# Edge sums of a graph transformer: masked out of PSUM by ScalarE, added in one VectorE operation; sort steps two slots apart

## What is computed

```
q, k, v = xp @ Wq, xp @ Wk, xp @ Wv                      # xp: normed rows with position and degree terms
att  = clip(einsum('ehd,ehd->eh', q[dst], k[src]) / scale, -50, 50)
ex   = exp(att - m[dst])
s    = segment_sum(ex, dst)                              # and the 6250 self edges
aggr = segment_sum(v[src] * ex / s[dst], dst)
x    = x + aggr @ Wo;   x = x + gelu(layernorm(x) @ W1) @ W2
```

## Time and profile before

| | us |
|---|---|
| median of 3 runs (3809.33 to 3823.78) | 3817.89 |
| the profiled execution, whole | 3814.57 |
| its span, first to last instruction | 3812.6 |
| granted TensorE clock, mean | 0.888 |

### The profile page before, as it was taken

The page is one execution under the profiler, slowest core; times in us unless marked ns, Lnnn a source line. Parts: engine busy times, 40 slices in busy tenths (PEclk is TensorE's granted clock), DMA queues, the critical chain, the costliest instruction groups (busy, mean ns, idle before and its releaser), DMA issues.

```text
span 3812.6 us, 74017 instructions
## 1 busy us (share of the span) xinstructions
PE 3120.4 (82%) x25398; PEld 2506.9 (66%) x25705; DVE 2896.4 (76%) x6187; ACT 1821.4 (48%) x4404; POOL 2513.6 (66%) x2470
## 2 busy tenths in 40 slices
PE   4984688888898888888887688888888888888887
PEld 3753566667676666776776476666666676766665
DVE  8995678777777877878787387778777777777776
ACT  1331245445354544545555345554555555555555
POOL 1007777677676766767676477776677777777772
PEclk6785789899898989989999799889998989999997
DMA  3024455445454544545454355554555555555552
GB/s 85 23 74 141 117 153 167 138 147 169 127 171 132 171 144 140 165 137 165 143 174 139 103 163 171 169 168 145 159 176 159 164 168 165 176 169 170 165 169 77
DMA packets 427248, 558.53 MB, mean 146 GB/s; under 512 B 78472, under 2 KB 345440, under 8 KB 426676
## 3 DMA queue, kind: packets, MB, share of 16 engines
q0 software_dynamic: 117504, 321.02, 28.7%
q1 hardware_dynamic: 301862, 225.47, 19.6%
q10 hardware_dynamic: 7506, 7.20, 0.6%
HBM read 527.98 MB, written 25.44 MB: 145 GB/s over the span
## 4 chain that ended last, share of the span: by engine, by line
PE 44%; DVE 25%; issue 8%; ACT 7%; POOL 6%; DMA 5%; SPq 2%; DVEq 1%; another core or an unknown queue 0%; POOLq 0%; ACTq 0%
PE psum L952 12%; PE psum L1042 6%; POOL kv_ring L1965 5%; PE psum L993 4%; PE psum L1026 4%; DVE att L1683 4%; PE psum L1063 2%; DVE scratch L1674 2%; PE psum L1009 2%; DVE work L1378 2%; DVE kv_ring L1395 2%; DMA q_win<-q_table 2%; PE psum L1123 2%; PE psum L970 2%; DVE scratch L1698 2%
## 5 line engine op out<-in xcount | busy, mean ns | idle before, releaser
L1965 POOL DMA_INDIRECT kv_ring<-kv_table,src_idx x1840 | 1878.1, 1021 | 732.9 <-issue 543.8
L1228 ACT ACTIVATE scratch<-psum 128x512 f32<-128x512 f32 (+1 forms) x1228 | 679.5, 568 | 553.0 <-PE psum L970 201.0
L1965 POOL DMA_INDIRECT arena<-kv_table,src_idx x608 | 617.2, 1015 | 273.5 <-issue 179.8
L952 PE MATMUL psum<-arena 128*128 128x256 f32 x2156 | 673.1, 435 | 73.1 <-ACT scratch L1228 43.9
L1239 ACT COPY arena<-psum 128x512 f32<-128x512 f32 x616 | 327.3, 532 | 580.5 <-PE psum L952 577.9
L993 PE MATMUL psum<-q_win,scratch 64*128 64x128 f32 x4896 | 410.0, 314 | 169.1 <-DVE scratch L1674 80.4
L952 PEld LDWEIGHTS psum<-arena 128*128 128x128 f32 x2156 | 422.9, 216 | 177.1 <-ACT scratch L1228 58.3
L1683 DVE TENSOR_REDUCE att<-scratch 128x64 f32<-128x1024 f32 (+1 forms) x460 | 536.0, 1165 | 0.1
L993 PEld LDWEIGHTS psum<-q_win,scratch 64*128 64x128 f32 x4896 | 346.8, 214 | 263.7 <-issue 166.5
L1009 PE MATMUL psum<-scratch 128*64 128x136 f32 x4896 | 373.2, 297 | 17.4 <-ACT work L1322 6.3
L1674 DVE TENSOR_TENSOR scratch<-psum,kv_ring 128x1024 f32<-128x1024 f32 x230 | 280.3, 1219 | 139.6 <-DMA kv_ring<-kv_table,src_idx 92.4
(11 more groups left out here) (252 smaller groups left out, 4725.0 us busy)
## 6 DMA issues: line engine op xcount, KB each, us to landing
arena<-kv_table SPq DMA_DIRECT2D x154, 896.0 KB
kv_ring<-kv_table,src_idx POOLq DMA_INDIRECT x1840
q_win<-q_table SPq DMA_DIRECT2D x612, 32.0 KB
work<-kv_table SPq DMA_DIRECT2D x98, 128.0 KB
q_win<-q_table SPq DMA_DIRECT2D x154, 64.0 KB
arena<-kv_table,src_idx POOLq DMA_INDIRECT x608
work<-q_table SPq DMA_DIRECT2D x98, 64.0 KB
kv_table<-work SPq DMA_DIRECT2D x49, 128.0 KB, 2.1
```

The source lines that it names most:

```text
L952: mm = e.matmul(to[:, t % 2 * 2 * D:(t % 2 + 1) * 2 * D], hot_source[:, t * P:(t + 1) * P], source_rows[:, t, :], start=True, stop=True)
L1228: e.activation(to[:, at:at + width], apart[k % FILL_BANKS][:, 0:width], ACT.Relu, bias=1.0, scale=-1.0).then_inc(apart_read, 1)
L1965: e.indirect_dma_start(kv[m % RING_KV][:, t, :], None, kv_table[l], bass.IndirectOffsetOnAxis(ap=src_idx[:, c * T + t:c * T + t + 1], axis ...
```

## The change

1. ScalarE gets `mask_sums`: for a chunk it waits for the sums, and writes sums times mask for both rows to a new tile `masked` (two buffers of 2 x 136 columns in `arena`), with two ACTIVATE operations. This stands in slot 2u+4 for unit u, behind the exp of unit u+2.
2. `add_sums` of a chunk is one TENSOR_TENSOR over both rows, 272 columns, `acc` plus `masked`, and moves from slot 2u+3 to slot 2u+5. Block adds keep slot 2u+3. The order of the adds is written out (`add_order`), and each waits for the one before.
3. `bank_free` of a bank that held a chunk's sums waits for `sum_masked` in place of `acc_added`.
4. Node steps of tiles fed by chunks start two slots later; each layer's list is two slots longer.
5. From sort 1 on, steps 5 to 18 of a sort are two slots apart. Sort 5 then stands in slots 194 to 231.

```diff
-        ready = 2 * LAYERS[l].last_unit(j) + 4 - SUMS
+        ready = 2 * LAYERS[l].last_unit(j) + (4 if j >= LAYERS[l].jb else 6) - SUMS
...
+SORT_EVERY = 2
...
             slots.setdefault(u, []).append((s, k))
-            u += 1
             if k in SORT_BANKED:
-                slots.setdefault(u, []).append((s, -k))
+                slots.setdefault(u + 1, []).append((s, -k))
+            u += SORT_EVERY if s and 5 <= k < SORT_STEPS - 4 else 1
...
-    return max(2 * LAYERS[l].nu + 2, len(node_steps(l)))
+    return max(2 * LAYERS[l].nu + 4, len(node_steps(l)))
...
-                if name == "edges":
+                if name == "edges" and LAYERS[l].is_block(j):
                     e.wait_ge(acc_added, adds[unit(l, j)])
+                elif name == "edges":
+                    e.wait_ge(sum_masked, 2 * (chunk(l, LAYERS[l].units[j][1]) + 1))
...
+        def mask_sums(e, l, u):
+
+            n, i = unit(l, u), LAYERS[l].units[u][1]
+            m = chunk(l, i)
+            e.wait_ge(edge_summed, n + 1)
+            if m >= 2:
+                e.wait_ge(acc_added, adds[chunk_unit(m - 2)])
+            for k in range(2):
+                e.activation(masked[:, m % 2, k, :], edge_sum(l, u), ACT.Identity, scale=in_block[:, k, i:i + 1]
+                             ).then_inc(sum_masked, 1)
...
                         make_exp(e, l, u)
+                    if slot % 2 == 0 and 2 <= u < LAYERS[l].nu + 2 and not LAYERS[l].is_block(u - 2):
+                        mask_sums(e, l, u - 2)
                     for fill_of in fills[2:]:
...
             what, i = LAYERS[l].units[u]
+            if adds[n] > 1:
+                e.wait_ge(acc_added, adds[n] - 1)
             if what == "chunk":
+                m = chunk(l, i)
                 block = e.value_load(block_ring[0:1, i:i + 1], min_val=0, max_val=RING_W - 1)
-            e.wait_ge(edge_summed, n + 1)
-            if n >= 1:
-                e.wait_ge(acc_added, adds[n - 1])
...
-                for k in range(2):
-                    row = two[:, k, :]
-                    e.scalar_tensor_tensor(out=row, in0=of_edges, scalar=in_block[:, k, i:i + 1], in1=row, op0=ALU.mult,
-                                           op1=ALU.add).then_inc(acc_added, 1)
+                e.tensor_tensor(two, two, masked[:, m % 2], ALU.add).then_inc(acc_added, 1)
                 return
...
-                        if u >= 1:
-                            add_sums(e, l, u - 1)
+                        for v in added_at(l, u):
+                            add_sums(e, l, v)
```

More of the change, by code:

```diff
@@ L97 @@
 EDGE_TILES = EP // P
-ARENA = 16656
+ARENA = 17200
 START_MAX = EDGE_TILES - ST
@@ L256, in sort_steps @@
             slots.setdefault(u, []).append((s, k))
-            u += 1
             if k in SORT_BANKED:
-                slots.setdefault(u, []).append((s, -k))
-        assert u + 2 <= 2 * at[s * OB] - 8
+                slots.setdefault(u + 1, []).append((s, -k))
+            u += SORT_EVERY if s and 5 <= k < SORT_STEPS - 4 else 1
+        assert u + 2 <= 2 * at[s * OB] - 8, (s, u, 2 * at[s * OB] - 8)
     return [slots.get(u, []) for u in range(max(slots, default=-1) + 1)]
@@ L367, in graph_transformer @@
         acc_b = part_of(HELD_B * MW).rearrange("p (w m) -> p w m", m=MW)
+        masked = part_of(2 * 2 * MW).rearrange("p (i k m) -> p i k m", i=2, k=2)
         source_rows = part_of(TB * 2 * D).rearrange("p (t d) -> p t d", t=TB)
@@ L534, in graph_transformer @@
         exp_ready, msg_ready = semaphore("exp_ready"), semaphore("msg_ready")
-        edge_summed, acc_added = semaphore("edge_summed"), semaphore("acc_added")
+        edge_summed, sum_masked, acc_added = semaphore("edge_summed"), semaphore("sum_masked"), semaphore("acc_added")
         own_in = [semaphore(f"own_in{i}") for i in range(WORK)]
@@ L630, in graph_transformer, with added_at @@
         of_chunk = [what == "chunk" for layer in LAYERS for what, _ in layer.units]
-        adds = [*itertools.accumulate(2 if chunk else 1 for chunk in of_chunk)]
+        def added_at(l, u):
+            return [v for v, block in ((u - 1, True), (u - 2, False)) if 0 <= v < LAYERS[l].nu and LAYERS[l].is_block(v) == block]
+        add_order = [unit(l, v) for l in range(L) for u in range(LAYERS[l].nu + 2) for v in added_at(l, u)]
+        adds = {n: k + 1 for k, n in enumerate(add_order)}
         q_loads = [sum(2 if of_chunk[m] else 1 for m in range(n % 2, n + 1, 2)) for n in range(units)]
@@ L1711, in add_sums @@
             what, i = LAYERS[l].units[u]
+            if adds[n] > 1:
+                e.wait_ge(acc_added, adds[n] - 1)
             if what == "chunk":
+                m = chunk(l, i)
                 block = e.value_load(block_ring[0:1, i:i + 1], min_val=0, max_val=RING_W - 1)
-            e.wait_ge(edge_summed, n + 1)
-            if n >= 1:
-                e.wait_ge(acc_added, adds[n - 1])
-            of_edges = edge_sum(l, u)
-            if what == "chunk":
+                e.wait_ge(sum_masked, 2 * (m + 1))
                 done = cleared_for(l, i)
@@ L1722, in add_sums @@
                 two = acc[:, bass.ds(block, 2), :]
-                for k in range(2):
-                    row = two[:, k, :]
-                    e.scalar_tensor_tensor(out=row, in0=of_edges, scalar=in_block[:, k, i:i + 1], in1=row, op0=ALU.mult,
-                                           op1=ALU.add).then_inc(acc_added, 1)
+                e.tensor_tensor(two, two, masked[:, m % 2], ALU.add).then_inc(acc_added, 1)
                 return
+            e.wait_ge(edge_summed, n + 1)
+            of_edges = edge_sum(l, u)
             row = acc_b[:, (i // OB) % HELD_B, :]
@@ L1910, in vector_edges @@
                             make_products(e, l, u + 1)
-                    elif slot % 2 == 1 and u <= LAYERS[l].nu:
+                    elif slot % 2 == 1:
                         if u < LAYERS[l].nu:
                             make_messages(e, l, u)
-                        if u >= 1:
-                            add_sums(e, l, u - 1)
+                        for v in added_at(l, u):
+                            add_sums(e, l, v)
                     for j, k in at(slots, slot):
```

## The result

| | before | after |
|---|---|---|
| median us (lowest, highest) | 3813.6 (3807.4, 3823.8) | 3892.4 (3882.4, 3898.0) |
| ratio, 95% interval | | 1.021 (1.018 to 1.024) |
| span of the profiled execution | 3812.6 | 3894.6 |
| first scores to last, layer 0 | 312.7 to 2089.5 | 311.8 to 2193.8 |
| of it the eight periods, units 34 to 202 | 1309.9 | 1415.8 |

The forecast was 3748 with a range up to 3815. Layer 0 lost 105 us, all in the eight periods that were to gain 79, and layer 1 gained 31.

The account below looks back on a forecast made before the run. POOL's gathers were taken to nearly bound layer 1; in layer 0 sort stretches ran slower than POOL, PE-bound free ones faster. Terms -79 - 11 + 1 + 12 + 4 + 3 = -70 gave 3745 profiled, 3748 us median, range 3690 to 3815.

Parts of the forecast that it names:

- the eight periods: Layer 0 from 619.5 us: eight stretches of 21 units, 163.7 us each on average, forecast to become 153.8.
- What bounds the kernel: POOL occupied 96% in layer 1 behind its sorts; layer 0 alternates; at most 137.8 us, 21.9 and 44.0 to gain.
- Sorts two slots apart, -79: Layer 0: one sort step in most units makes a unit 7.32 us, saving 9.9 us in each of eight periods.
- the waiting of 9.8 us a sort: Sort 5 in layer 0: 9.8 of its 29.2 us cost is waiting within a slot, not PE's work.
- the second rival: Sort steps: their cost is additive, so spreading brings nothing; 3803 us, chance 0.13.
- The 31.2 us that I put beside the 9.8: Placing matmuls' waits, read as sort 5's, mostly for DVE steps of the slot just before: 31.2 us.
- One add on DVE, -9: One 424 ns add replaces two of 352, sparing DVE 0.28 us a chunk; counted for 97 layer 1 chunks.
- Two masks on ACT, +10: Masks of 0.36 us each, 0.72 a chunk on ACT; by its chain share, +10 us for 97 layer 1 chunks.
- Banks, nothing: Chunk banks read a slot later, 52 wanted in that slot and 97 one later; wait costed at nothing.
- The fourth rival: PE waits for banks in 149 places; 3852 us at 0.7 us each; chance 0.12.
- Ends and node steps, +3: Ends of both layers get two more slots but no work of note: +3 us together, bounds 0 and +8.
- The lock, +16: New add with two SBUF inputs shuts out POOL, 0.08 us a chunk: +12 in layer 1, +4 in layer 0.

Follow-up runs that it names:

- the one pair measured: Masks ahead of the exp, sorts one slot apart: 3832.6 us with the block's add first, 3753.1 with the chunk's add first.
- the chunk's add first: Chunk's add ahead of the block's, against the kernel with masks ahead of the exp and sorts one slot apart (3832.6 us): 3753.1 us, 0.984 of before.
- adds and bank a slot later: Kernel before with later node steps (3762.9 us), plus a chunk's two old DVE adds one slot later, no masks on ACT: 3815.7 us, 1.001 of before.
- masks alone: The change with sorts one slot apart, keeping items 1 to 4: 3868.8 us, 1.012 of before; 0.9665 and 0.9682 with TensorE starved.

## Why the prediction was wrong

- **What bounds the kernel.** That POOL is a near bound and leaves at most some 66 us in layer 1 and 138 in layer 0 held: in all eight kernels with the later node steps POOL's waits in layer 1 fell to 0.3 to 12.7 us and the layer to 1580 to 1609 us. The best kernel still left 62 us of POOL's waits in its periods.
- **Sorts two slots apart, -79.** The main failure. Alone they gave -21 in the eight periods (-17 in the median), and +16 to +30 together with later node steps. I took a unit's cost to be its free time plus PE's share of the sort, 7.32 us, with the waiting of 9.8 us a sort gone. That is the step that failed: alone, such a chunk unit took 8.47, which is free time plus half of what two steps had added, as in the second rival. The waiting did not go; it went along with the steps. It stands in the units with a read-out (10.55, and 14.79 in the change, against 7.02 and 6.87 without), where VectorE needs what TensorE has just made; that this hand-over is the cause is read from the distances and not tried by itself. The 31.2 us that I put beside the 9.8 were those of all eight sorts; in sort 5 the placing matmuls waited 4.1. The granted clock did go the forecast way with the spread alone, to 0.94.
- **One add on DVE, -9.** The operation was sized right, what it saves was too high (0.18 us a chunk and not 0.28, as the old adds overlapped), and its waits were wrong. I wrote that the new add, a slot later, will not wait. It no longer waits for sums but for the block's add queued ahead of it on DVE, 112 us in 140 places. The full diff has both, `added_at` with the block first and the new wait ahead of `value_load`; I named what is queued behind the new waits of ACT and not those of DVE. Step missing, worth 80 us in the one pair measured.
- **Two masks on ACT, +10.** A mask was sized right (0.366 us), a pair takes 0.63 us of busy time and not 0.72 (191.7 us for 306); nothing in the runs calls for more than that from ACT's load. Their place behind the exp is worth 30 to 36 us, through the bank.
- **Banks, nothing.** This was the second failure. The fourth rival had the mechanism, at 0.7 us a reuse and 104 in all; measured without masks, and with the adds' place on VectorE in it, it is 53. In the change PE waits 89 us for masks in the periods. My reason against it, that PE is behind DVE, is true of waits for sums and not of a ring in which each late read stops whichever matmul comes third.
- **Ends and node steps, +3.** The two ends cost 9 us (60.7 + 40.0 where it was 53.8 + 38.1). I counted the later node steps at the ends only. They move every such node step against the edge work, its loads and stores on SP too, and the line alone gains 54 us. The forecast had no term for that gain, and it hides part of what the other terms missed.
- **The lock, +16.** The new add does shut out POOL: of 100 gathers that began during it 77 took over 1.05 us, with a mean of 1.104, where those that began while DVE was idle took 0.945: 16 us in all; before, none of 68 that began during the old adds did. In the time the term isn't seen. In layer 1, POOL-bound in all three, the mean gather is 1.043 us with the old adds and later node steps (912.2 + 321.0 us for 1182), 1.044 in the change (911.3 + 322.2) and 1.032 with the chunk's add first (916.9 + 302.7). Later node steps, with no new add, had already brought it there from the 1.015 before.

The signs that I had named came out against me: periods of 173 to 186 us and not 154, POOL's waits in layer 0 at 268 and not 60, PE's clock at 0.88 and not 0.95, and PE idle for masks, 89 us in the periods. The mean gather rose to 1.024 (forecast 1.03, below the 1.05 that would have told against it).

From before to the change the kernels measured make a chain: -54 with node steps later, +53 with adds and bank a slot later, +53 from there to masks alone (masks, new add, and the adds' order in one), +24 with the spread. That they add up to 3893 is no test of the account, since each step begins where the last one ends. The last two are differences between runs, not causes by themselves.

## What to carry to other kernels

A list written out for five engines has to be read again in full for every line that moves: what the moved step is queued behind, what is queued behind it, and who gets the buffer it now holds longer. Here three parts of the same diff were worth -54, +53 and +80 us, and the operation that it was about, 0.18 us saved in each of 306 places, was small beside them. Spreading work over more slots brought little: a unit with one step cost half of what two had added, waiting included. Waiting that is to go away should first be traced to the hand-over that it belongs to. The version with masks ahead of the exp, the chunk's add first and sorts one slot apart took 3753 us, 0.984 of before, and beats both kernels; node steps later alone gives 3763. The intervals of these two overlap (0.981 to 0.987, 0.982 to 0.988), so no run shows that masks and the single add gain anything over the one line.

## What the hardware showed that I had not expected

- The same kernel before took 3814 to 3817 us on some chips and 5361 to 5365 on others. On the latter PE's idle time with no visible wait was 780 us where it was 4, and its busy time 3731 us where it was 3155 (masks alone on both), and the change was worth -3.3% there and +2.1% on the others.
- A VectorE operation behind a semaphore wait and then a register load began 0.79 us after the operation that it waited for had ended. The copy at 1197.76 in the same timeline, with its waits and no register load, began 0.26 us after the operation ahead of it. How the 0.79 divides was not tried.
- Of 340 gathers that began in the kernel before while messages were made from two SBUF operands (L1698), 270 took over 1.05 us; of 391 that began during products with a PSUM operand (L1674), none did.
- The granted clock in the sort periods fell from 0.92 to 0.88 as PE's waits rose, and PE's busy time there rose by 72 us (1136.6 to 1208.2), some 16 us of it because before has 1.4% fewer matmul records (8866 against 8988). A wait on PE may be paid a second time, in its clock; that this is cause and effect wasn't tried by itself, and masks alone speaks against a general rule: its periods are 60 us longer than before, with 72 us of waits for masks, at an unchanged 0.92.
